# Mixture-of-experts layer with residuals: the shared expert as its own phase over row pairs, gate and up by a seven-product scheme

## What is computed

```python
def _gemma_mlp(x, gate_w, up_w, down_w):      # gate_w, up_w: 256 x 1024, down_w: 1024 x 256
    g = einsum('bsh,hi->bsi', x, gate_w)
    u = einsum('bsh,hi->bsi', x, up_w)
    return einsum('bsi,ih->bsh', gelu(g, approximate=True) * u, down_w)

w, sel = top_k(softmax(router_logits), 2)      # router_logits = cond_8, 8 rows x 8 experts
w = w / w.sum(axis=-1, keepdims=True)
out = sum over the 2 chosen experts of w * _gemma_mlp(x, skill_gate[e], skill_up[e], skill_down[e])
x = x + out + _gemma_mlp(x, shared_gate, shared_up, shared_down)
x = x + x @ W_base.T + b_base + 2.0 * sum over e of cond_8[b, e] * (x @ As[e].T) @ Bs[e].T
```

## Time and profile before

| what | value |
|---|---|
| runs | 847.97, 848.79, 853.68 us, median 848.79 |
| profiled execution, span from the first to the last instruction | 848.9 us |
| own time of that execution | nothing to speak of beyond the span: 0.1 us over the median of the runs |
| matmuls | 3766, of which 3456 have 512 columns |
| bytes moved | 62.95 MB, 74 GB/s over the span |

### The profile page before, as it was taken

One profiled execution on the slowest core, in us unless ns is written; L12 is line 12 of the kernel. 1 busy time (PEld: TensorE's weight loads), 2 busy tenths in 40 slices (PEclk: granted clock), 3 DMA queues, 4 the chain that ended last, 5 costly groups with the idle time before them and its releaser, 6 DMA issues.

```text
span 848.9 us, 10976 instructions
## 1 busy us (share of the span) xinstructions
PE 828.7 (98%) x3766; PEld 689.6 (81%) x3766; DVE 464.5 (55%) x682; ACT 360.6 (42%) x583; POOL 9.2 (1%) x20
## 2 busy tenths in 40 slices
PE   4899999999999999999999999999999999999997
PEld 3688888888888888888888888888888888888886
DVE  3764645555555555646465554564645646455553
ACT  2654433444344434344344444343534444334442
POOL 4000000000000000000000000000000000000000
PEclk9899999999999999999999999999999999999999
DMA  5642311414032230322303131132221313013000
GB/s 154 218 136 65 96 42 44 131 43 132 0 95 78 74 99 0 99 74 74 99 9 127 37 110 63 37 99 72 76 62 37 127 46 104 8 49 126 1 1 25
DMA packets 59651, 62.95 MB, mean 74 GB/s; under 512 B 4144, under 2 KB 56368, under 8 KB 59632
## 3 DMA queue, kind: packets, MB, share of 16 engines
q1 hardware_dynamic: 58944, 61.88, 23.3%
q0 software_dynamic: 544, 0.79, 0.4%
q10 hardware_dynamic: 144, 0.03, 0.0%
HBM read 58.49 MB, written 4.19 MB: 74 GB/s over the span
## 4 chain that ended last, share of the span: by engine, by line
PE 96%; DMA 2%; ACT 0%; SPq 0%; DVE 0%; issue 0%; DVEq 0%
PE ps_acc L278 31%; PE ps_gate L278 31%; PE ps_up L278 31%; PE ps_misc L278 4%; DMA raw_dn<-_L_cond_shared_down_dram 2%; PE ps_misc L315 1%; DVE x_lo L500 0%; ACT L448 0%; SPq L200 0%; ACT sh_gu_hi L411 0%; SPq L199 0%; DVE x L581 0%; DVE o_row L597 0%; ACT x_hi L411 0%; ACT gelu L448 0%
## 5 line engine op out<-in xcount | busy, mean ns | idle before, releaser
L411 ACT CAST inner_hi<-inner 128x512 fp32r<-128x512 f32 x192 | 119.2, 621 | 315.5 <-DVE inner L617 201.6
L500 DVE TENSOR_TENSOR inner_lo<-inner,inner_hi 128x512 fp32r<-128x512 f32 x192 | 133.0, 693 | 129.3 <-ACT inner_hi L411 129.3
L617 DVE SCALAR_TENSOR_TENSOR inner<-gelu,coef_now,ps_up 128x512 f32<-128x512 f32 x128 | 95.6, 747 | 135.0 <-PE ps_up L278 135.0
L448 ACT ACTIVATE gelu<-ps_gate 128x512 f32<-128x512 f32 x192 | 114.2, 595 | 115.6 <-PE ps_gate L278 115.0
L500 DVE TENSOR_TENSOR ex_gu_lo<-raw_gu,ex_gu_hi 128x1024 fp32r<-128x1024 f32 x64 | 78.5, 1226 | 49.4 <-ACT ex_dn_hi L411 49.4
L278 PE MATMUL ps_gate<-x_cur_hi,ex_gu_hi 128*128 128x512 f32 x256 | 100.3, 392 | 0.0
L278 PE MATMUL ps_acc<-inner_hi,ex_dn_lo 128*128 128x512 f32 x256 | 99.7, 389 | 0.0
L278 PE MATMUL ps_gate<-x_cur_lo,ex_gu_hi 128*128 128x512 f32 x256 | 99.7, 389 | 0.0
L278 PE MATMUL ps_acc<-inner_hi,ex_dn_hi 128*128 128x512 f32 x256 | 99.7, 389 | 0.0
L278 PE MATMUL ps_gate<-x_cur_hi,ex_gu_lo 128*128 128x512 f32 x256 | 99.6, 389 | 0.0
L278 PE MATMUL ps_up<-x_cur_hi,ex_gu_hi 128*128 128x512 f32 x256 | 99.6, 389 | 0.0
(11 more groups left out here) (95 smaller groups left out, 1177.5 us busy)
## 6 DMA issues: line engine op xcount, KB each, us to landing
raw_gu<-n_L_cond_skill_gate_dram SPq DMA_DIRECT2D x64, 256.0 KB, 2.8
raw_gu<-in_L_cond_skill_up_dram SPq DMA_DIRECT2D x64, 256.0 KB, 3.4
raw_dn<-n_L_cond_skill_down_dram SPq DMA_DIRECT2D x64, 256.0 KB, 3.7
x_nat<-in_x_dram SPq DMA_DIRECT2D x8, 512.0 KB, 4.7
out_dram<-o_row SPq DMA_DIRECT2D x16, 256.0 KB, 3.9
raw_gu<-_L_cond_shared_gate_dram SPq DMA_DIRECT2D x4, 256.0 KB, 14.6
raw_gu<-in_L_cond_shared_up_dram SPq DMA_DIRECT2D x4, 256.0 KB, 14.8
raw_dn<-_L_cond_shared_down_dram SPq DMA_DIRECT2D x4, 256.0 KB, 16.2
```

The costliest lines, as they stand in the source:

```text
L411: return nc.scalar.copy(dst, src)
L448: nc.scalar.activation(gelu[:, k % 2, :], ps_gate[k % 2][:], ACT.Gelu_apprx_tanh).then_inc(gelu_done, 1)
L500: return V.tensor_tensor(dst, src, hi.bitcast(F32), ALU.subtract)
L617: V.scalar_tensor_tensor(out=inner[:, k % 2, :], in0=gelu[:, k % 2, :], scalar=coef_now[:, s:s + 1], in1=ps_up[k % 2][:], op0=ALU.mult, op ...
```

## The change

The shared expert leaves the rows. It becomes a phase of its own ahead of them: 4 pairs of rows (q), and in each 4 pairs of weight columns (j), 16 units u. In a unit, gate and up are each a 2 x 2 block product: rows r by column halves, over two channel chunks. It is computed with 7 block products for 8: `left` holds the weight blocks and their sums (made by GpSimd, split by ScalarE and VectorE) in the tile `wide`, `right` the blocks of x and their differences in `xc`. Three of the products add into a bank in which another one stands already, after ScalarE has copied the bank out (`copy_out`). VectorE (`first_sum`, `off_diagonal`) and GpSimd (`outputs`) put the four output blocks together. The down product is as before, 8 block products for a unit, into four banks.

The transposed x of every row and the shared expert's result go out to scratch in DRAM (`xt_dram`, `sh_dram`). The second phase has 16 steps for a row, over the two chosen experts only; SP brings x and the result of a row back, and GpSimd adds them (`base`). The SBUF of the first phase is used again by the second. x of the next row is split into another buffer instead of being copied at the row's end.

Cut to its core:

```diff
-    SLOTS = 1 + TOP_K
-    K = SLOTS * IC
+    K = TOP_K * IC
+    Q = B // 2
+    NU = Q * PAIRS
+A11, A12, A22, S1, S2, S3, S4 = range(7)
+B11, B21, B22, T1, T2, T3, T4 = range(7)
+PRODUCTS = [(0, A11, B11, True), (2, S1, T1, True), (3, S3, T3, True), (1, S2, T2, True),
+            (0, A12, B21, False), (2, S4, B22, False), (3, A22, T4, False)]
...
+            sp.dma_start(x_nat, x_rows[0]).then_inc(x_landed[0], 16)
+            sp.dma_start(raw_part(0, GATE), sg[:, :, 0:PW]).then_inc(gate0_landed, 16)
+            sp.dma_start(x_nat1, x_rows[1]).then_inc(x_landed[1], 16)
...
+            sp.wait_ge(right_ready, rights(Q - 1, NP - 1))
+            sp.wait_ge(right_hi, rights(Q - 1, NP - 1))
+            sp.wait_ge(xt_stored, 16 * B)
+            sp.dma_start(xf_first, xt_dram[0]).then_inc(x0_landed, 16)
...
+            def outputs(u, part, to):
+                m = 2 * u + part
+                pool.wait_ge(copied, 3 * m + 3)
+                G.tensor_tensor(v57, v57, p7, ALU.add).then_inc(v_done, 1)
+                pool.wait_ge(v_done, m + 1)
+                pool.wait_ge(u1_done, m + 1)
...
+                G.tensor_tensor(to, v57, u1, ALU.add).then_inc(c22_done, 1)
...
+            def matrix(u, part):
+                q, j = divmod(u, PAIRS)
+                m = 2 * u + part
+                for n, (bank, a, b, opens) in enumerate(PRODUCTS):
...
+                    if n == 0 and part == UP:
+                        pe.wait_ge(sh_gelu, 4 * u + 1)
+                    elif n == 0 and u > 0:
+                        pe.wait_ge(sh_mul, 3 * (u - 1) + 1)
+                    elif n == 1 and m > 0:
+                        pe.wait_ge(c_done, 2 * (m - 1) + 1)
+                    elif n == 2 and m > 0:
+                        pe.wait_ge(c_done, 2 * (m - 1) + 2)
+                    elif n == 3:
+                        if m > 0:
+                            pe.wait_ge(u1_done, m)
...
+                    elif n >= 4:
+                        pe.wait_ge(copied, 3 * m + n - 3)
+                    product(ring[bank][:], [left(j, hl, part, a) for hl in range(2)],
+                            [right(q, hl, b) for hl in range(2)], opens, True, not opens)\
+                        .then_inc(product_done, 1)
...
+            for u in range(NU):
+                q, j = divmod(u, PAIRS)
+                matrix(u, GATE)
...
+                if u > 0:
...
+                    shared_down_part(u - 1, 0)
+                matrix(u, UP)
+                if u > 0:
+                    shared_down_part(u - 1, 1)
...
+            def copy_out(m, n, to, bank):
+                act.wait_ge(product_done, products(m, n))
+                if n == 0 and m > 0:
+                    act.wait_ge(c_done, 2 * m)
+                    act.wait_ge(c22_done, m)
+                nc.scalar.copy(to, ring[bank][:]).then_inc(copied, 1)
...
+            for u in range(NU):
+                q, j = divmod(u, PAIRS)
+                qn = q + 1
+                if qn < Q and j in (1, 2):
+                    take_xt(qn, 0 if j == 1 else 2, ring[1])
+                copy_out(2 * u, 0, u1, 0)
+                if q > 0 and j == 1:
+                    acc0_to_stage(q - 1)
+                copy_out(2 * u, 1, v57, 2)
+                copy_out(2 * u, 2, p7, 3)
+                shared_gelu(u)
...
+                if q == 0 and j < PAIRS - 1:
+                    act.wait_ge(sh_landed[j + 1], 48)
+                    split_left(j + 1, (j + 1) % 2, slice(0, 2))
+                    split_a22(j + 1, (j + 1) % 2, slice(0, 2))
+                    split_sums(j + 1, slice(0, 2), j + 3)
+                    split_shared_down(j + 1)
...
+                copy_out(2 * u + 1, 0, u1, 0)
+                copy_out(2 * u + 1, 1, v57, 2)
+                copy_out(2 * u + 1, 2, p7, 3)
+                shared_inner_hi(u)
+                if qn < Q and j == 2:
+                    act.wait_ge(t_made, 4 * q + 1)
+                    split_right(qn, T1, t_a)
+                    act.wait_ge(t_made, 4 * q + 2)
+                    split_right(qn, T3, t_b)
+                if qn < Q and j == 3:
+                    act.wait_ge(t_made, 4 * q + 4)
+                    split_right(qn, T4, t_a)
...
+                first_sum(2 * u + 1)
+                shared_mul(u, 0)
+                off_diagonal(u, UP, 0)
+                off_diagonal(u, UP, 1)
+                shared_mul(u, 1)
+                shared_inner_lo(u, 0)
+                shared_mul(u, 2)
+                shared_inner_lo(u, 1)
+                shared_inner_lo(u, 2)
+                shared_inner_lo(u, 3)
...
+            row(0, 0, True)
+            with pe.Fori(0, (B - 2) // 2) as i:
+                row(i * 2 + 1, 1, False)
+                row(i * 2 + 2, 0, False)
+            row(B - 1, 1, False)
+            layer1(B - 1)
```

More of the change, by code:

```diff
@@ L122, in cond_resid_kernel @@
         coef_now = sb("coef_now", [P, 3])
[L123 to L128, removed]
-        raw_landed = [sem(f"raw_landed{j}") for j in range(PAIRS)]
-        x_landed = sem("x_landed")
+        ring = [psum(f"ps_ring{i}") for i in range(4)]
+        acc = [[psum(f"ps_acc{b}{m}") for m in range(HC)] for b in range(2)]
@@ L272, in _ @@
+            row(0, True)
+            with pool.Fori(0, B - 1) as i:
+                row(i + 1, False)
         @block.tensor
         def _(pe):
-            def product(dst, left, right, start, stop):
-                passes = [(0, 0), (0, 1), (1, 0)]
-                for n, (a, b) in enumerate(passes):
-                    last = pe.matmul(dst, left[a], right[b], start=start and n == 0,
-                                     stop=stop and n == len(passes) - 1)
-                return last
-            def weights_of(k):
-                gu, dn = (sh_gu, sh_dn) if k < IC else (ex_gu, ex_dn)
-                return gu, dn, k % IC // 2
@@ L287, in project @@
[L287 to L300 removed]
+            PASSES = [(0, 0), (0, 1), (1, 0)]
@@ L302, in down, with project @@
+            def project(par, k, dst, part):
+                j, p = k % IC // 2, k % 2
+                for c in range(HC):
+                    last = product(dst[:], [ex_gu(hl, j, part, c, p) for hl in range(2)],
+                                   [x_cur(par, hl)[:, c * S:(c + 1) * S] for hl in range(2)],
+                                   c == 0, c == HC - 1)
+                return last
+            def down(b, k):
+                j, p = k % IC // 2, k % 2
                 pe.wait_ge(inner_ready, b * K + k + 1)
@@ L303, in down @@
                 for m in range(HC):
-                    last = product(ps_acc[m][:], [w[:, j, k % 2, m * P:(m + 1) * P] for w in dn],
+                    last = product(ps_acc[m][:], [ex_dn(hl, j, p, m) for hl in range(2)],
                                    [v[:, k % 3, :] for v in inner_s], k == 0, k == K - 1)
@@ new lines, in row @@
+                    if k in (0, 2):
+                        j = 2 + k // 2
+                        if first:
+                            split_routed(b, 0, j, product_done, products(2 * (NU - PAIRS + j) + 1, NP - 1))
+                        else:
+                            split_routed(b, 0, j, down_done, b * K - K + IC + 2 * j + 2)
+                    elif k % 2 == 0 and k < 12:
+                        split_routed(b, 1, k // 2 - 2, down_done, b * K + k - 2)
+                    elif k % 2 == 0 and not last:
+                        split_routed(b + 1, 0, k // 2 - 6, down_done, b * K + k - 2)
```

889 lines of the change are left out of this document (637 added, 252 removed).

## The result

The changed kernel takes 866.44 us (865.17 to 867.66), the kernel before 849.33 in the same comparison: a ratio of 1.0186, 95% interval 1.0159 to 1.0214. It is slower by 1.9%, where 835 us and a gain were forecast. The profiled execution took 865.17 us, with a span of 863.4 us, 14.5 more than before. The times are 17.1 us apart. In every run that has both, the time is 1.8 to 2.1 us above the span, so the span of 848.9 us before belongs, by my estimate, to an execution of about 850.7 us, and not to the median, as the prediction took it. Spans are compared with spans from here on.

A forecast was written before the change was run, and what follows sets the result against it. The prediction took the number of TensorE matmuls to bound the kernel: 848.9 less 21.8 for 96 matmuls, plus 6 for unit stalls, 0 for the start and 1 for passing over gave 834.1, stated as 835 us, range 829 to 853.

The forecast's parts named there:

- rival 4: Matmuls: adding into an opened bank or the wide operand spaces them further apart, 845 us; chance 0.25 together with Rival 1.
- hand schedule of a plain unit: Shared-phase unit: operation times counted on VectorE and ScalarE, leaving 1.1 us to spare before product 4.
- the wait named as the tightest: Each unit: product 4 adds into bank 0 only after ScalarE has copied it out; wanted at 17.68 us, copied at 16.6.
- the stall term of the units: Shared phase: PE stalls from late ScalarE and VectorE work, likely between 2.4 and 9.6 us, taken as 6.
- The lock: Units: VectorE and GpSimd may block each other on SBUF; second multiply 0.86 us late, stall term up to 9.6 us.
- (a): ScalarE's transposed-x copy in second and third units, a T4 cast before the first: no stall; about 0.25 us six times if locked.
- (b): Second units of row pairs 1 to 3: ps_acc stage copies delay bank 2's copy, 0.3 us twice; 1.1, 1.1, 0.6 if locked.
- (c): Casts of T1 and T3 before the fourth unit: 1.04 us, just in time; 0.75 us three times if locked.
- the start: Start up to matmul 63, put at about 36 us against about 37 before: difference 0, bounds -2 to +4 us.
- passing over and routed rows: Change to the routed phase, scratch traffic and routed rows, row boundary densest: +1 us for all, 0 to +4.
- rival 2: Units: GpSimd becomes the bound, each growing by 3P - 6.2 us (P one GpSimd operation); above 857 us, chance 0.13.
- Rival 1: Vector side gives the gain back, 853.7 us at full sum, milder mixture 842 to 850; chance 0.25 together with rival 4.

The follow-up runs named there:

- late casts alone: Changed kernel with ScalarE's T1 and T3 casts and the stage copies moved behind the bank copies: 860.97 us, ratio 1.0120 to the kernel before.
- all four changes: Changed kernel with early x load, fold one step earlier, fourth-quarter product on VectorE, and casts and stage copies behind bank copies: 842.24 us, ratio 0.9898.
- The last experiment: The kernel with all four changes, plus the first unit's up-weight casts moved behind the gate matrix's three bank copies: 841.66 us, ratio 0.9913.
- eight products: Changed kernel's own shared phase, but gate and up by 8 block products, without GpSimd sums or bank copies, x early: 851.94 us; fold one step earlier too: 848.12.

## Why the prediction was wrong

**What held.** 96 matmuls went, and the spacing of the others did not change (rival 4 is out). A GpSimd sum takes 1.30 us, for my 1.2. The hand schedule of a plain unit was right to a tenth: from the up matrix's start at 188.72 us I had VectorE's operations (a sum, a multiply, a sum, a multiply and the first inner_lo) at 2.88, 3.56, 4.24, 5.53 and 6.14 us behind it, and they stand at 2.93, 3.66, 4.34, 5.63 and 6.23. Then inner_lo takes 1.79, and the third multiply stands at 7.94 for 6.75, 1.2 us late. The tail is unchanged. And the wait named as the tightest, product 4 for a bank copy, is what PE waited for most.

**The step that failed first: the stall term of the units, 6 us with 9.6 as its upper end.** Units 1 to 15 have 26.0 us of excess. Three things were wrong in it.

- The lock. I had it as one possibility, priced as 0.86 us at the second multiply. It is real, and in 15 of 16 units it falls on the inner_lo behind that multiply with 1.1 us, since that operation meets GpSimd's product nearly whole; in the other one it falls on the multiply, with 1.0. Taking the product out, or onto VectorE, takes 10 us out of units 4 to 15 and 9 to 12 out of the span. I took the middle between no lock and full lock. The rule pointed to the upper end, and nothing in the trace pointed to the lower one.
- The need for bank 1. Only product 4 was on my list. Product 3 writes bank 1, where the transposed x still stands in second and third units; it waits for ScalarE's copy L724, which stands behind four casts: 3.2 us in six waits, and 3.4 in one wait once x came early.
- Ends that meet. I priced (a), (b), (c) and the lock each on a unit that began on time. In the fourth unit of the first two row pairs the lock, an x copy in unit three, and two casts come one after the other in ScalarE's queue: 4.7 and 4.0 us where I had 0.75 at most. Without the product they are 3.8 and 1.6, with the late casts alone 3.8 and 1.8, with all four changes 1.5 and 0.9. Behind those stops of 3.0 and 2.3 us, five matmuls each go 0.43 us apart, another 1.0 us each, and the granted clock is at its lower level, 0.50:

```profile
81.20:84.40 3.20, 2.92 (x7) 0.50 0.00 0
149.50:152.70 3.20, 2.94 (x7) 0.50 0.00 0
```

Behind the other stops from unit 1 to the last routed row, of 1.3 us and less, no matmul is that slow. I had no term for that.

**The second step: the start, 0 with +4 as its upper end.** The 63rd matmul of 512 columns, the one that the prediction counted to, starts at 45.46 us for 36.99, 8.5 us later (it lies in unit 1, and the 2.6 us of excess up to it there are in the 26.0 as well). I followed ScalarE's and VectorE's queues and the bytes, and not SP's: x of row 2 is wanted at the end of unit 0, and its load stands behind two waits for weight splits. It is issued at 32.2 us, and PE stands for 5.4 us; then eleven matmuls go 0.43 us apart, at a granted clock of 0.50. In the first row pair as a whole, moving the load saves 3.2 us, as the next wait is right behind it. Another stop, of 3.5 us at 20.35, stands in the first gate matrix: the copies that free its banks stand in ScalarE's queue behind the casts of the up weights, which wait for a transfer and for GpSimd's sums until 18.9 us. The prediction had that gate matrix end near 21; it ends at 25.5. The last experiment took this stop out and won 1.9 us of excess.

**The third: passing over and routed rows, +1 with 0 to +4.** Routed rows have 9.1 us of excess, 1.1 of it in a stop at the passing over and 6.3 in seven stops of 0.9 us. I called the beginning of a row its densest place and found it covered, which it is: GpSimd's add of 1024 columns makes no stop there, although it too holds up one inner_lo in each row change (2.30 to 2.57 us for 0.69). The stop is at the end, where two steps of cover have run out because the last down product waits for its own step. The shorter row put the w_eff split into a step with a weight split.

**The rivals.** The result lies in rival 2's range of times, but not by its mechanism: GpSimd's operations of 512 columns never reached 2 us, and its product was ready before ScalarE wanted it. Rival 1, the vector side giving the gain back, names the mechanism, and its full sum, 853.7, was 9.7 us short of the span: too little for units and start, nothing for the clock. What I gave 0.25 as "no change" was the right story with its sizes too small.

**A slip.** The prediction lets the shared phase end at about 235 us. Sixteen units are 239.4 us of matmuls alone, behind a first product at 10.5. It ended at 302 us. No term of the sum uses the 235.

**What stays open.** The first row pair still has 22.7 us of excess in the best version, for 9.1 with eight products; how much of it is GpSimd's S blocks meeting VectorE's splits was not taken apart.

## What to carry to other kernels

A scheme that trades matmuls for elementwise work is paid for in the order of the other engines' queues, long before these are full: here 21.8 us of matmuls to be won became 17 us lost with VectorE 65% and ScalarE 50% busy, and 8 us won after four moves that left the matmuls alone. When work goes to GpSimd, list VectorE's operations with two SBUF inputs that stand at the same moment and add a whole GpSimd operation to each; one more operation on the busier VectorE can be cheaper. And for each bank list every product that waits for it, and for each transfer everything that SP's queue holds ahead of it.

## What was not expected of the hardware

The lock's two-sidedness, with numbers of these runs: a VectorE operation of 512 columns with two SBUF inputs takes 0.68 us alone, up to 1.79 beside a GpSimd product and up to 2.57 beside GpSimd's add of 1024 columns; GpSimd's product 1.29 where it was first and 1.74 where VectorE was; VectorE's operations that read a bank, 0.69, beside either. From the groups of the changed kernel, GpSimd on 512 and on 1024 columns (mean ns):

```profile
L448 POOL TENSOR_TENSOR post<-post 128x512 f32<-128x512 f32 x32 | 41.9, 1309 | 103.7 <-ACT post L774 90.5 <-DVE post L1018 13.1
...
L493 POOL TENSOR_TENSOR post<-post 128x1024 f32<-128x1024 f32 x8 | 19.3, 2406 | 468.6 <-DMA post<-sh_scratch 461.9 <-DMA post<-xt_scratch 6.6
```

The select row that served as a bound, 2.2 ns a column for one input, turned out to be the pace for two inputs as well (2406 - 1309 = 1097 ns for 512 columns more).
